# Two shared tiles moved to the end of the last expert stage, and tokens scattered in two halves

## The reference

```
logits = xt @ gate_w.T
scores = softmax(logits)
_, indices = top_k(scores + gate_bias, 2)
weights = take_along_axis(scores, indices, axis=1)
combine = (one_hot(indices, 8) * weights[..., None]).sum(axis=1)
for e in range(8):
    y = y + mlp(xt, w1[e], w2[e], w3[e]) * combine[:, e:e + 1]
z = mlp(xt, sw1, sw2, sw3)            # the shared expert, every token
x = x + tanh(g_ffn[1]) * (y + z)      # xt = layernorm(x)
mlp(x, w1, w2, w3) = (silu(x @ w1.T) * (x @ w3.T)) @ w2.T     # 256 -> 512 -> 256
```

## Time and profile before

| | us |
|---|---|
| median of 3 runs | 3183.37 |
| profiled execution, its own time | 3195.05 |
| span of the profiled execution | 3193.4 |
| start of the stage (first `m_t`) | 2648.3 |
| last routed tile turned | 3148.1 |
| first copy to `out` issued | 3178.07 |
| mean granted clock of TensorE | 0.972 |

### The profile page before, as it was taken

How to read it: one execution, slowest core, us unless ns; L and a number is a source line. 1 busy time by engine, 2 the same in 40 slices (tenths; PEclk the granted TensorE clock), 3 DMA queues, 4 the chain that set the end, 5 groups by cost and what they waited for, 6 DMA issues and landing times. The chain is left out here.

```text
span 3193.4 us, 48431 instructions
## 1 busy us (share of the span) xinstructions
PE 2961.9 (93%) x18056; PEld 2395.0 (75%) x18056; DVE 2218.2 (69%) x3785; ACT 1808.8 (57%) x2899; POOL 1266.6 (40%) x866
## 2 busy tenths in 40 slices
PE   5999999999999999999969958999999968999996
PEld 5888888788887888878859944555555438899996
DVE  6777777777777777776745547777777545478885
ACT  3555555555555555555535526888888843366664
POOL 2111111111111111111124427888887724468885
PEclk9999999999999999999979978999999988999998
DMA  8101010010100101000035644334433123268886
GB/s 263 38 11 34 11 37 11 17 34 11 37 11 17 34 11 37 11 16 21 5 113 202 213 122 134 106 120 120 119 115 100 41 80 113 86 180 237 232 231 170
DMA packets 201740, 279.23 MB, mean 87 GB/s; under 512 B 18035, under 2 KB 139538, under 8 KB 201456
## 3 DMA queue, kind: packets, MB, share of 16 engines
q1 hardware_dynamic: 182864, 245.48, 24.1%
q0 software_dynamic: 18656, 30.82, 5.0%
HBM read 194.50 MB, written 85.87 MB: 88 GB/s over the span
## 5 line engine op out<-in xcount | busy, mean ns | idle before, releaser
L309 POOL TENSOR_TENSOR a_w_stage<-a_w_stage,a_consts 128x256 f32<-128x256 f32 x64 | 39.5, 617 | 1231.7 <-PE a_scores L36 1196.4
L1673 POOL TENSOR_TENSOR c_pT_lo<-c_prob,c_pT_hi 128x1024 fp32r<-128x1024 f32 x192 | 456.2, 2383 | 113.5 <-ACT c_pT_hi L1756 109.4
L395 ACT ACTIVATE a_prob<-a_scores,a_neg_max 128x1024 f32<-128x1024 f32 x256 | 286.1, 1117 | 362.4 <-DVE a_neg_max L493 359.2
L493 DVE TENSOR_REDUCE a_neg_max<-a_scores 128x1 f32<-128x1024 f32 x256 | 310.1, 1211 | 109.9 <-PE a_scores L36 107.2
L388 ACT ACTIVATE a_pT_hi<-a_probT 128x512 fp32r<-128x512 f32 x512 | 279.1, 598 | 188.0 <-PE a_probT L732 187.9
L1868 DVE TENSOR_REDUCE c_neg_max<-c_max 128x2 f32<-128x1024 f32 x248 | 302.1, 1218 | 69.4 <-PE c_max L2101 68.3
L440 DVE TENSOR_TENSOR a_pT_lo<-a_probT,a_pT_hi 128x512 fp32r<-128x512 f32 x512 | 327.4, 681 | 20.8 <-ACT a_pT_hi L388 20.8
L1750 ACT ACTIVATE c_prob<-c_scores 128x1024 f32<-128x1024 f32 x256 | 261.0, 1020 | 70.7 <-PE c_scores L2112 66.6
L732 PE MATMUL a_probT<-k_ident,a_prob 128*128 128x128 f32 x2048 | 268.5, 273 | 17.5 <-DVE a_pT_lo L440 17.5
L732 PEld LDWEIGHTS a_probT<-k_ident,a_prob 128*128 128x128 f32 x2048 | 233.0, 140 | 43.2 <-issue 22.6
L34 PE MATMUL m_h<-m_rT_hi,m_w_hi 128*128 128x256 f32 x880 | 255.2, 290 | 3.4 <-DVE m_rT_lo L2588 1.9
(11 more groups left out here) (339 smaller groups left out, 8524.9 us busy)
## 6 DMA issues: line engine op xcount, KB each, us to landing
m_w_in<-L_ffn_w_in SPq DMA_DIRECT2D x117, 512.0 KB
e_w_in<-L_ffn_w_in SPq DMA_DIRECT2D x32, 1024.0 KB, 6.9
qk_dram<-c_stage SPq DMA_DIRECT2D x64, 256.0 KB
c_q_rows<-qk_dram SPq DMA_DIRECT2D x32, 512.0 KB, 5.0
c_k_rows<-qk_dram SPq DMA_DIRECT2D x32, 512.0 KB, 5.8
rows_in_dram<-a_blank SPq DMA_DIRECT2D x1, 10062.0 KB, 38.9
m_row_in<-rows_in_dram SPq DMA_DIRECT2D x39, 258.0 KB
a_w_stage<-L_xattn_Wq_in SPq DMA_DIRECT2D x64, 128.0 KB, 2.2
```

The lines of the kernel that those rows point to most:

```text
L395: a(prob[:, qt, :], ps_s[:, qt % 2, :], ACT.Exp, bias=neg_max[:, qt:qt + 1], accum_out=row_sum[:, par, qt:qt + 1]).then_inc(exp_done, 1)
L493: ve.tensor_reduce(neg_max[:, qt:qt + 1], ps_s[:, qt % 2, :], AX.X, ALU.max, negate=True).then_inc(max_done, 1)
L1673: g.tensor_tensor(flat(pT[1][:, kt - 1]), flat(prob[:, kt]), flat(pT[0][:, kt - 1]).bitcast(F32), ALU.subtract).then_inc(lo_pool, 1)
```

## The change

Of the 16 shared tiles the last two (tokens 3584 to 4095) are taken from before the routed tiles and put behind them. NA is now 14, the routed tiles are 14 to 52, and the shared tiles FIRST = 53 and LAST = 54 come last.

- The scatter: the groups are 5, 5, 5, 5, 6, 6 for the first choice and 5, 5, 6, 5, 5, 6 for the second, over 12 tiles where there were 14. `scattered` is two semaphores, one for each half of the 32 token groups; DVE changes the weight column by halves, behind tiles 4 and 6, and POOL's second choice waits for the first half, then for the second.
- The residual of tiles 53 and 54 goes to `sums` at the start of the stage (two more stores on SP), so that routed results are added to it.
- The shared weights are loaded a second time as weight number 40, with the same splits on ACT, POOL and DVE as those of a routed tile.
- PE makes the second product of tile 52 right behind that of tile 51, and DVE its result, so that the last `add` can go.
- Behind the last `add` SP brings the rows of the two tiles back from `sums` into `acc`, and copies the other 3584 tokens in seven DMAs of 0.5 MB. DVE adds the two shared results to what came back, and ACT stores them to `out` from its own queue.

```
-        NA = B * S // R1
+        NS = B * S // R1
+        NA = NS - 2
+        HALF = NT // 2
...
+        FIRST = NA + NR
+        LAST = NS + NR - 1
...
             dma(blank_v, z[:, 0:RT, 0:D]).then_inc(kept, 16)
+            for j in range(NA, NS):
+                dma(sums_v[:, j], acc[:, RT * j:RT * j + RT]).then_inc(kept, 16)
...
-            sp.wait_ge(scattered, 16 * TOP * NT)
+            for half in range(2):
+                sp.wait_ge(scattered[half], 16 * TOP * HALF)
...
-            for n in range(NA + 3, LAST + 1):
+            for n in range(NA + 3, FIRST):
                 bring(n)
+            sp.wait_ge(w_lo, 2 * NR - 2)
+            for j in range(2):
+                load(0, j, shared_views[j])
+            sp.wait_ge(w2_lo, NR)
+            load(0, 2, shared_views[2])
             sp.wait_ge(summed, 16 * RT * NR)
-            for i in range(0, B * S, B * S // 4):
-                part = slice(i, i + B * S // 4)
+            for j in range(NA, NS):
+                dma(acc[:, RT * j:RT * j + RT], sums_v[:, j]).then_inc(back, 16)
+            for i in range(0, NA * R1, S):
+                part = slice(i, i + S)
...
-            for n, count in enumerate((4, 4, 4, 5, 5, 5, 5)):
+            for n, count in enumerate((5, 5, 5, 5, 6, 6)):
...
-            pool.wait_ge(second_weight, 1)
             first = 0
-            for n, count in enumerate((5, 5, 5, 5, 4, 4, 4)):
-                pool.wait_ge(t_full, n + 8)
+            for n, count in enumerate((5, 5, 6, 5, 5, 6)):
+                pool.wait_ge(t_full, n + 7)
+                pool.wait_ge(second_weight, 1 if n < 3 else 2)
...
+            for n in (FIRST, LAST):
+                act.wait_ge(o_out, n + 1)
+                j = n - NR
+                nc.scalar.dma_start(out_rows[R1 * j:R1 * j + R1].rearrange("(t p) d -> p t d", p=P), acc[:, tokens(n)]).then_inc(last_stored, 16)
+            act.wait_ge(last_stored, 32)
...
-                if n:
+                if n and n not in (FIRST, LAST):
                     result(n - 1)
-                if n == 7:
-
-                    dve.wait_ge(scattered, 16 * NT)
-                    ve.tensor_copy(z[:, :, D + 1:D + 2].rearrange("p t o -> p (t o)"), weight[:]).then_inc(second_weight, 1)
+                if n == FIRST - 1:
+                    result(n)
+                if n in (4, 6):
+
+                    half = n // 6
+                    part = slice(HALF * half, HALF * half + HALF)
+                    dve.wait_ge(scattered[half], 16 * HALF)
+                    ve.tensor_copy(z[:, part, D + 1:D + 2].rearrange("p t o -> p (t o)"), weight[:, part]).then_inc(second_weight, 1)
+            dve.wait_ge(back, 32)
+            result(FIRST)
             result(LAST)
...
-                if n:
+                if n and n != FIRST:
                     second_product(n - 1)
+                if n == FIRST - 1:
+                    second_product(n)
```

More of the change, by code:

```diff
@@ L2392, in layer1_experts @@
         o_full, o_out = sem("o_full"), sem("o_out")
-        kept, summed, out_stored = sem("kept"), sem("summed"), sem("out_stored")
-        LAST = NA + NR - 1
+        kept, summed, back, out_stored, last_stored = (sem(n) for n in ("kept", "summed", "back", "out_stored", "last_stored"))
+        FIRST = NA + NR
+        LAST = NS + NR - 1
         views = [v.rearrange("e (c p) f -> p e c f", p=P) for v in (w1_d, w3_d, w2_d)]
@@ L2398, in layer1_experts @@
         sums_v = sums[0:B * S].rearrange("(j t p) d -> p j t d", t=RT, p=P)
+        shared_views = ffn.shared_views
         blank_v = sums[B * S:].rearrange("(t p) d -> p t d", p=P)
         out_rows = out_dram.rearrange("b s d -> (b s) d")
-        assert NA % 2 == 0
+        assert NA % 2 == 0 and NR % 2 == 1 and LAST == FIRST + 1
         def number(n):
-            return max(n - NA + 1, 0)
+            return min(max(n - NA + 1, 0), NR + 1)
         def routed(n):
-            return n >= NA
+            return NA <= n < FIRST
         def tokens(n):
-            return slice(RT * n, RT * n + RT)
+            j = n if n < NA else n - NR
+            return slice(RT * j, RT * j + RT)
         def product(n, f):
@@ L2417, in high @@
         def high(m, j):
-            return {0: (1, 2, 3), 1: (4, 5, 8)}[m][j] if m < 2 else 3 * m + (0, 1, 5 if m < NR else 3)[j]
+            return {0: (1, 2, 3), 1: (4, 5, 8)}[m][j] if m < 2 else 3 * m + (0, 1, 5 if m <= NR else 3)[j]
         block = ctx.enter_context(nc.Block())
@@ L2495, in add @@
                 if n == NA:
-                    pool.wait_ge(kept, 16 * (NA + 1))
+                    pool.wait_ge(kept, 16 * (1 + NS))
                 else:
@@ L2517, in _ @@
                 first += count
[L2518 to L2523, removed]
+                if n in (3, 4):
+                    low(1, n - 3)
+            for n in range(NA, FIRST):
+                low(number(n + 1), 0)
+                low(number(n + 1), 1)
                 if n >= NA + 2:
                     add(n - 2)
-            add(LAST - 1)
-            add(LAST)
+            add(FIRST - 2)
+            add(FIRST - 1)
         @block.scalar
@@ L2561, in _ @@
                 m = number(n)
-                ahead = routed(n) and n < LAST
-                if ahead:
+                if routed(n):
                     split(m + 1, 0)
@@ L2576, in _ @@
                 hidden_high(n, 3)
-                if routed(n):
+                if routed(n) or n == FIRST:
                     split_w2(m)
```

9 lines of the change are left out of this document (5 added, 4 removed).

## The result

| | before | after |
|---|---|---|
| median of 6 runs, us | 3183.4 (3176.84 to 3184.75) | 3167.65 (3163.21 to 3173.09) |
| profiled execution, its own time | 3195.05 | 3166.34 |
| its span | 3193.4 | 3164.7 |
| last pair of adds starts | 3172.59 | 3141.72 |
| mean granted clock of TensorE | 0.972 | 0.975 |

The ratio of the runs is 0.9956, with a 95% interval of 0.9943 to 0.9969: 14 us faster by the ratio (9.9 to 18.1), 15.8 by the medians. The forecast was 3169.7, range 3155 to 3178. The profiled executions differ by twice as much, 28.7 us. So two things are to be explained: the gain in the runs, and why the two profiles show double.

What follows compares the result with a forecast made beforehand. PE's work was taken to bound the stage up to 3166, the serial adds and the copy its end. Span 3193.4 to 3179.7 gives 13.7 us less: 3183.4 - 13.7 = 3169.7, range 3155 to 3178.

Steps and rivals of the forecast that it cites:

- The base: Whole kernel before: median 3183.37 us, profile 11.7 us above it; the tail's difference is carried over to the median.
- accident: Shared tiles turned from 2725.67 to 2757.06: 13.4 us lost in the profiled execution, which the median mostly lacks.
- Rival 1: Shared tiles: the burst of scatters starves PE in timed runs too, halves cure it; 13.4 us more, 3156.3; chance 0.17.
- The adds: POOL's last three adds, held by landing alone, 6.33 us apart; all sums done at 3162.2, 15.9 us earlier.
- The copy and the stores: End: copy at 3.0 us per MB, done at 3178.2; last two stores beside it add 1.5 us, ending at 3179.7.
- rival 2: End: half-size copies cost a microsecond each, or stores wait behind the copy; 3 to 10 us, 3173 to 3180; chance 0.11.
- PE at the end: Second product of tile 52: low hidden parts about a microsecond late, 0.8 us added; bounds 0 and 2 us.
- a wait of more than 2 us at tile 52: Sign of being wrong: PE waiting at tile 14, 52 or 53 for more than 2 us.
- over 16 would have been wrong: Sign of being wrong: tail from PE's last matmul to the end over 16 us, where 12.5 was said.
- The head: Start of stage: scatters issued by 2753, POOL waits 3 us, rows in time for tile 14 at 2770.7; cost 0.
- Rival 3: Head: rows of tile 14 come late, costing from 5 us of delay on; 3194 for 25 us; chance 0.05.
- The sum: Whole kernel: span 3179.7 against 3193.4, 13.7 us less; on the median, 3169.7.

Runs made afterwards that it cites:

- e2: The kernel before with only the weight column changed by halves, behind tiles 5 and 7, no tile moved: 3180.88 us, ratio 0.9951.
- f4: The kernel before, column still changed once, with the second choice's scatters in groups of 6, 6, 5, 5, 5, 5 behind tiles 9 to 14: 3180.7 us, ratio 0.9954.
- f1: The changed kernel itself, one sum written in another order, on the second chip, where before takes 3194.83: 3169.55 us, ratio 0.9916.
- f2: The changed kernel with one copy of 3.5 MB at the end in place of seven: 3172.2 us, ratio 0.9924.
- e4: The changed kernel with four shared tiles at the end instead of two, six copies, scatters squeezed into ten tiles: 3174.03 us, ratio 0.9928.
- f3: The changed kernel with the add of tile 50 ahead of both low parts of weight 40 on POOL: 3175.48 us, ratio 0.9935.
- e3: The changed kernel with the whole weight column changed once behind tile 7, as before had it: 3191.26 us, ratio 0.9985.
- e1: The kernel before with nothing of its work changed, one sum written in another order: 3194.13 us, ratio 0.9993.
- g1: The changed kernel once more, on the third chip, where before takes 3179.69: 3167.02 us, ratio 0.9962.
- g2: The changed kernel with the add of tile 50 between the two low parts of weight 40 on POOL: 3168.31 us, ratio 0.9962.

## Why the prediction was right, and where it was not

**The base: right as a number, wrong as a reading.** The 13.4 us lost at the shared tiles were called an accident of the execution. They aren't: on two of these three chips before runs at 3195, and never under 3192 (26 runs), and taking the burst away returns 14.7 us (e2) and 14.1 (f4). But the runs of before in the result, at 3183, are like those of the third chip, at 3180, and the profile of before, at 3195, is like the other two. The profile of the changed kernel is again like the third chip: it has 15 scatters in a row at the head, and no tile behind them is late. So the two profiles differ by 28.7 us because one is of the one kind and one of the other. That the runs of the record mostly lack the loss was right; "mostly" and "accident" should have been "on this chip" and "burst". Rival 1, given 0.17, had the mechanism right, and its 27 us are what f1 shows (25.3); its time of 3156 was wrong, since the runs of the result mostly lack the loss. What was said against it was half sound: the profile did stand 11.7 us above the median, but that groups of 5 did nothing to PE says nothing of 15. There is no trace of before on the third chip; that it doesn't starve there is read from its time alone. And each chip was used on one occasion: what is called a chip here may be an occasion.

**The adds: right.** Foreseen 6.33 us apart and 15.9 us earlier; they are 6.52 and 6.47 apart and, counted from the first turned tile and without the 13.4 us, the last is 18.1 us earlier, 15.5 without the 2.6 of the routed tiles (see the sum). They are released by landings, and SP went on 5.62 us behind the start of the last (5.48 said).

**The copy and the stores: right.** From the landing of the last add to the end, 17.5 us were forecast, 17.4 are measured (3147.34 to 3164.7). 3.0 us per MB held at half the size, and f2 shows that the cut makes no difference; rival 2's cost for each copy is out. The stores end the span 1.5 us behind the copies, the size given to them. Their 11 us from issue to landing are not their own length: the last store of e4, behind the copies, landed in 2.6 us. They share busy DMA engines (0.85, 283 GB/s). The rule of the Trainium skill, DMA: Bandwidth & Descriptors, issuing engines are not separate DMA queues, says the same: ACT's queue would save issue time on SP, not transfer time. No run here has the stores on SP.

**PE at the end: the mis-sized term.** 0.8 us was set for the second product of tile 52, bound 2; it waited 2.14. The reason given, late hidden parts, was not it: PE waited for the low part of the weights on DVE. By the forecast's own words a wait of more than 2 us at tile 52 would show it wrong, and this sign did come, by 0.14 us. It cost little or nothing: the last matmul ends at 3152.6, and the tail behind it is 12.1 us (12.5 said, over 16 would have been wrong). In f3 the term grew to 5.97 us and PE ended 14.3 us behind the start of the last add instead of 10.9, yet the end came 22.6 us behind it, no later than the 23.0 here. What f3 lost at the end, it lost because the same low part held back a result that an add needed. Only when four tiles stand at the end (e4) is PE's end the bound.

**The head: right.** POOL waits 1.6 to 2.9 us ahead of each group from the fourth on (3 said ahead of the second choice, 1.6 measured; 0.5 ahead of the last two, which follow a `low`), and never for the column, the last scatter is issued at 2752.0 (by 2753 said), the rows are loaded at 2760.84 (2759.5), and tile 14 is turned at 2771.29 (2770.7), with no wait. Rival 3 never showed. Even in e3, with the last scatter at 2776.9, the rows came in time, because PE was late itself.

**The sum.** Counted from the stage's first turned tile (2648.35 before, 2648.95 after), the profiled stage is 29.3 us shorter: 13.4 of starvation, and 15.9. Of these, 13.7 were forecast. The rest lies in the routed tiles: their 38 steps took 345.8 us before (turned at 2801.93 and 3147.74) and 343.2 after (2771.29 and 3114.53). Over all traces with the old end they take 343.1 to 347.4 us, over those with two tiles at the end 342.7 to 345.1, so it may be spread between executions; without it 13.3 us are left of the 15.9. Why it spreads, no run tells.

**Still open.** What in a run of scatters holds PE. It is not bandwidth (100 GB/s, while routed tiles run at 228 to 248 with PE full), and no semaphore that the profile shows; PE's idle time is put down to issue. Nor does the length of the run settle the price alone: 10 in a row cost 1.6 us at the head of f1 and 11 cost 4.2 at that of e4, where 15 behind a pause of 18 us cost 13.8 in e1. What sets the chips, or the occasions, apart is open too. The Trainium skill, Runtime: NRT & Kernel Launch, instruction fetch mechanics, says that an engine's instructions are fetched in blocks by DMA, mostly hidden; a fetch that scatters delay would look like this. The DMA packets of the traces speak against it. On the queue marked as instruction (q8) a packet of 16 KB comes for every 250 or so matmuls and weight loads of PE, and none in the whole span of before or e1 takes longer than 1.7 us. In e1 one starts at 2732.6 and takes 1.1 us, and the next starts at 2760.9; in between PE stands again and again up to 2745.7, and no packet of that kind lands. It runs 244 instructions between the two starts (206 to 292 between others of the stage), so it had them at hand while it stood. What the trace doesn't show is the time from the request of a fetch to its start.

## What to carry to other kernels

Before a stretch in which the profile differs from the median is called an accident, run the same kernel again elsewhere: a loss can be in every run of one chip and in none of another, and its cause can be cured by the way the work is dealt out. Deal indirect DMAs out in small groups: here five at a time, with some 2 us between the groups, cost nothing anywhere, six cost up to 0.9 us and seven 1.4 to 1.9 in spite of the pause. A wait ahead of them is worth avoiding less for itself than for the burst that it piles up. When a serial chain of DMAs with a copy behind it ends a kernel, put independent work after its last producer, and check which engine's work the shifted chain will now meet.

## What the runs showed of the hardware

- A burst of indirect DMAs on GpSimd (one each 1.28 us) took TensorE from 78 matmuls in 9 us to 13 (15 in a row, e1) and 6 (21 in a row, e3), from 7.4 to 8.2 us behind its first scatter on; 15 in a row did nothing on another chip (g1). PE stood idle between its matmuls, and the granted clock fell to 0.54 (e1) and 0.50 (e3) over a window, near 1.2 GHz; in the window behind, with PE at work again, it was still 0.70 and 0.56.
- VectorE's tensor_tensor of 128x1024 took 1.22 us alone, 4.36 us beside one (g2) and 6.37 us beside two (f3) such operations on GpSimd, which themselves took 2.9 us each beside it and 2.4 alone. It ended 1.1 us behind the last of them, though by the trace it had started 0.1 to 0.4 us ahead of the first of them.
- Two accumulating indirect DMAs (128 rows each) that wait for the landing of the two before cost 6.3 to 6.5 us a pair, of which 1.55 us each is GpSimd's own time.
